# Two-layer directed graph network over 16 graphs: the mean is subtracted ahead of the closing root, and layer 1 spreads its row maxima one projection earlier

## What is computed

```
h = max(layernorm(x), 0)
for each of two layers:
    a    = softmax(h h^T / sqrt(384)) * adj
    attn = a / (rowsum(a) + 1e-10)
    ctx  = (attn above the diagonal) (h Wl^T + bl) + diag(attn) (h Ws^T + bs) + (attn below it) (h Wr^T + br)
    h    = max(layernorm(ctx) * g + beta, 0)
out = x + h
```

## Time and profile before

| | us |
|---|---|
| median of 3 runs | 1187.16 (1187.15 to 1187.18) |
| profiled execution, its own time | 1188.02 |
| its span in the profile | 1186.3 |
| TensorE busy | 1169.5 (99%) |
| VectorE busy | 1004.8 (85%) |
| GpSimd busy | 633.0 (53%) |
| ScalarE busy | 494.5 (42%) |

### The profile page before, as it was taken

The page is one execution under the profiler, slowest core; times in us unless marked ns, Lnnn a source line. Parts: engine busy times, 40 slices in busy tenths (PEclk is TensorE's granted clock), DMA queues, the critical chain, the costliest instruction groups (busy, mean ns, idle before and its releaser), DMA issues.

```text
span 1186.3 us, 18757 instructions
## 1 busy us (share of the span) xinstructions
PE 1169.5 (99%) x6998; PEld 1157.7 (98%) x6998; DVE 1004.8 (85%) x2064; ACT 494.5 (42%) x1065; POOL 633.0 (53%) x669
## 2 busy tenths in 40 slices
PE   9999999999999999999999999999999999999997
PEld 7999999999999999999999999999999999999997
DVE  6879987799877998779997798977989779895688
ACT  5346423364343543435434343344433454335532
POOL 3676454654545555455564455654556544654347
PEclk9999999999999999999999999999999999999999
DMA  6521312013120131211312112121222113110000
GB/s 226 203 65 54 115 54 81 19 54 116 54 81 19 54 115 55 80 36 55 97 54 81 37 63 90 58 76 37 83 70 80 54 36 104 48 54 1 1 27 27
DMA packets 43483, 80.57 MB, mean 68 GB/s; under 512 B 6912, under 2 KB 24832, under 8 KB 43392
## 3 DMA queue, kind: packets, MB, share of 16 engines
q1 hardware_dynamic: 43104, 78.98, 20.0%
q10 hardware_dynamic: 288, 0.39, 0.1%
HBM read 66.72 MB, written 12.64 MB: 67 GB/s over the span
## 4 chain that ended last, share of the span: by engine, by line
PE 54%; DVE 20%; POOL 10%; issue 10%; ACT 4%; DMA 1%; DVEq 0%; POOLq 0%
PE u_ps L337 9%; PE u_ps L339 9%; PE u_ps L338 9%; PE rot_ps L339 8%; PE rot_ps L338 8%; PE rot_ps L337 8%; POOL dg L957 4%; POOL hw_lo L945 4%; DVE et_lo L682 3%; DVE e_sb L677 3%; DVE xt_sb L665 3%; DVE proj L710 2%; DVE z L747 2%; DVE z L755 2%; ACT e_sb L515 2%
## 5 line engine op out<-in xcount | busy, mean ns | idle before, releaser
L945 POOL TENSOR_TENSOR hw_lo<-proj,hw_hi 128x384 fp32r<-128x384 f32 x256 | 283.1, 1126 | 242.3 <-ACT hw_hi L525 242.3
L337 PE MATMUL rot_ps<-w_hi,ht_hi 128*128 128x384 f32 x1152 | 389.3, 338 | 0.0
L339 PE MATMUL rot_ps<-w_hi,ht_lo 128*128 128x384 f32 x1152 | 385.4, 335 | 0.0
L338 PE MATMUL rot_ps<-w_lo,ht_hi 128*128 128x384 f32 x1152 | 385.2, 334 | 0.0
L338 PEld LDWEIGHTS rot_ps<-w_lo,ht_hi 128*128 128x128 f32 x1152 | 216.6, 188 | 0.0
L337 PEld LDWEIGHTS rot_ps<-w_hi,ht_hi 128*128 128x128 f32 x1152 | 216.5, 188 | 0.0
L339 PEld LDWEIGHTS rot_ps<-w_hi,ht_lo 128*128 128x128 f32 x1152 | 216.3, 188 | 0.0
L500 ACT ACTIVATE u_off<-u_ps 128x128 f32<-128x128 f32 (+1 forms) x128 | 42.4, 332 | 395.6 <-PE u_ps L339 395.4
L525 ACT ACTIVATE hw_hi<-proj 128x384 fp32r<-128x384 f32 x256 | 127.5, 520 | 78.1 <-DVE proj L710 78.1
L957 POOL TENSOR_TENSOR dg<-et_hi,tri 128x256 fp32r<-128x256 f32 x128 | 109.7, 857 | 89.9 <-PE u_ps L339 89.9
L710 DVE TENSOR_TENSOR proj<-rot_ps,bias 128x384 f32<-128x384 f32 x256 | 137.8, 548 | 21.9 <-PE rot_ps L339 21.8
(11 more groups left out here) (89 smaller groups left out, 2100.6 us busy)
## 6 DMA issues: line engine op xcount, KB each, us to landing
out_dram<-z SPq DMA_DIRECT2D x64, 192.0 KB, 1.9
x_norm<-x_dram SPq DMA_DIRECT2D x15, 768.0 KB, 4.5
xt_sb<-x_t_dram SPq DMA_DIRECT2D x15, 768.0 KB, 4.5
adj_a<-adj_t_dram SPq DMA_DIRECT2D x8, 1024.0 KB, 5.3
adj_b<-adj_t_dram SPq DMA_DIRECT2D x8, 1024.0 KB, 5.4
x_norm<-rows_dram SPq DMA_DIRECT2D x15, 512.0 KB, 3.8
x_a<-x_dram SPq DMA_DIRECT2D x8, 768.0 KB, 4.6
x_b<-x_dram SPq DMA_DIRECT2D x8, 768.0 KB, 4.7
```

The costliest lines, as they stand in the source:

```text
L337: pe.matmul(dst, a_hi, b_hi, start=first and m == 0, stop=False)
L338: pe.matmul(dst[:, 0:b_lo.shape[1]], a_hi, b_lo, start=False, stop=False)
L339: done = pe.matmul(dst, a_lo, b_hi, start=False, stop=last and m == n - 1)
L945: pool.tensor_tensor(hw_lo[:, t, n, :], proj[:, t % 2, n, :], hw_hi[:, t, n, 0:dim].bitcast(F32), ALU.subtract).then_inc(hw_lo_done, 1)
```

## The change

Four edits. In the unit list of layer 1, M stands behind three projections, (0,0), (0,1), (1,0), where it stood behind four. ScalarE copies the spread maxima before it rounds tile 0's projections. VectorE shifts the scores of tiles 0 and 1 before it reads out projection (1,1). GpSimd, in steps 1 and 3, does `x_centre` before `rstd_of`. No instruction is added or taken away.

```diff
-    UNITS_1 = [("P", *p) for p in PROJ[:4]] + [("M",)] + [("P", *p) for p in PROJ[4:] + SELF]
+    UNITS_1 = [("P", *p) for p in PROJ[:3]] + [("M",)] + [("P", *p) for p in PROJ[3:] + SELF]
...
                     for t in range(TILES):
                         row_sum(t)
+                    copy_max()
                     round_proj(0)
-                    copy_max()
                     exp(0)
...
                     evacuate(1, 0)
-                    evacuate(1, 1)
                     shift_scores(0)
                     shift_scores(1)
+                    evacuate(1, 1)
                     evacuate(2, 0)
...
-                rstd_of(slice(0, TILES), 1)
                 if s in (1, 3) and not last:
                     x_centre(it * 2 + (2 if s == 1 else 3))
+                rstd_of(slice(0, TILES), 1)
```

## The result

| | before | changed |
|---|---|---|
| median | 1187.17 us (6 runs, 1187.13 to 1187.80) | 1180.28 us (6 runs, 1179.88 to 1181.25) |
| profiled execution, its span | 1188.02, 1186.3 | 1179.88, 1178.1 |

The ratio is 0.9942, 95% interval 0.9929 to 0.9955: faster by 6.9 us, where 6.6 was forecast.

The account below looks back on a forecast made before the run. TensorE, busy 99% of the span, was taken as the bound. Terms of -3.85 (wait B), -3.85 (wait A), -0.1 (last pair) and +1.2 (M in step 3) gave -6.6 us: 1180.6 us, range 1179.0 to 1184.2.

Parts of the forecast that it names:

- What bounds: Whole kernel: TensorE is busy 99% of the span, so only its waits can be won, or new ones added.
- waits A and B: TensorE's waits, seven times 0.55 us each: A, step 2's transposes for a bank; B, step 0 for low parts.
- The subtraction ahead of the root costs nothing: Steps 1 and 3: GpSimd's 4.25 us of subtraction fit its 5.92 us idle gap, ending 1.7 us before `var_eps`.
- Wait B goes: Step 0 of the next pair: GpSimd's low parts end 2 us earlier, where 0.5 is needed; 7 x 0.55 = -3.85 us.
- Start of step 2: `x_scale` takes 1.88 us, VectorE waits for projection (0,0), and the maxima are 0.42 us ahead of M.
- How wait A goes: Step 2: earlier M and shifts give the read-out of (2,0) 0.75 us of lead; 7 x 0.55 = -3.85 us.
- M in step 3: Moved one projection earlier, M waits for the maxima 0.15 us in each of eight step 3: +1.2 us.
- The remainder of A in the last pair: Turns of step 2 in the last pair: a remaining wait of 0.1 us goes.
- Rival 1: Step 3: A's gain is given back to M, up to 0.55 us in seven pairs; 1184.4 at worst; chance 0.14.
- Rival 2: M becomes the bound in both steps, waiting 1.1 us in step 2; about 1188.2, no change; chance 0.05.
- Rival 3: The root waits behind the subtraction for the spread means; slower, 1194.5 with the load 2 us beyond slack; chance 0.03.
- Rival 4: The change does not reach TensorE: A and B find other releases just as late; 1188.4; chance 0.04.

Follow-up runs that it names:

- e3: The kernel before, with the mean subtracted ahead of the root in step 1 only; 1184.06 us, ratio 0.9975.
- e4: The kernel before, with the mean subtracted ahead of the root in step 3 only; 1183.92 us, ratio 0.9971.
- e1: The kernel before, with only the mean subtracted ahead of the root in steps 1 and 3; 1180.30 us, ratio 0.9942.
- e6: The changed kernel with ScalarE's copy and VectorE's read-out of (1,1) in their old orders; 1180.21 us, ratio 0.9941.
- e2: The changed kernel with the mean subtracted behind the root again, as before; 1191.44 us, ratio 1.0036.
- e8: e1 plus four unused GpSimd subtractions of 128x384 that read SBUF, behind the root of step 2; 1200.49 us, ratio 1.0111.

## Why the prediction was right

- **What bounds.** Right: waits A and B were all there was between the first pair and the tail, and e3 and e4 give each its size, 0.50 us (0.08 of A stays as long as M is not moved) and 0.54, for 0.55 read from the rows.
- **The subtraction ahead of the root costs nothing.** Right, with 2.17 and 1.54 us to spare for the 1.7 forecast. The `centre` beside it is stretched by 0.3 us, within the 1.4 allowed. In the first pair the root comes 1.1 us later, for up to 1.6 forecast, and nothing follows from it; but it is held by way of VectorE's `den`, not by GpSimd's own queue as the prediction had it.
- **Wait B goes.** Right; GpSimd's chain has 2.2 us of lead on the product, so it gained some 2.7, where I had estimated 2.
- **Start of step 2.** Right in what follows the change: scaling 1.89 us, VectorE waits 1.73 us for projection (0,0), the maxima are 0.4 us ahead of M. But the prediction had VectorE late by 2.2 us, from `x_scale` alone, and by contention. It was 3.4 us: `shift` was held for 1.1 us too, and much of the lateness of `x_scale` can be its dependence on the subtractions. As the change removes all of it, the sum did not suffer.
- **How wait A goes.** Here the reasoning credits the wrong edit. The prediction had A go by the lead that the earlier M and the earlier shifts give to the read-out of (2,0). e1 has neither, and A shrinks from 0.55 to 0.08 us all the same; e6 has the old order of copy and shifts, and A is gone. The moved subtraction is what removes A; the earlier M takes the last 0.08. The size of the term was right, since the change has both edits.
- **M in step 3.** The mechanism was right; the term was oversized. I had 8 x 0.15 = 1.2 us. Measured are 0.10 us each, and 0.27 in one pair: 1.0. The prediction took 0.14 us from an instruction's end to the start that it releases, from wait B; from the last maximum to M it is 0.06.
- **The remainder of A in the last pair** was 0.1 us, as forecast, and it too is gone.
- **The sum.** -6.6 forecast, -6.9 measured; the difference is less than two executions differ by at their start.

Rival 1 (A given back in step 3) did not happen: in the change M of step 3 starts 0.23 us after the matmul before it, and 0.22 in e2, where A is freed by M's own wait in step 2. Rival 2 did not happen here, but its price was about right: e2, without the moved subtraction, shows M's wait of 1.0 us in step 2, for 1.1. Rival 3 did not happen; both roots wait for `var_eps`. Rival 4 did not either: e3 and e4 show that each wait reaches the time. The chances of rivals 2 and 4 add up to 0.09, where the prediction put 0.08 for the two. What the prediction did not say, though its numbers held it, is that one of the four edits carries the whole gain: with the subtraction moved, what the earlier M wins in the turns (0.08 us a pair) and what it loses in step 3 (0.10) cancel.

What the runs do not settle: how much of VectorE's lateness in step 2, and so of wait A, was the collision and how much the dependence of `x_scale` on the subtractions; and what sets the differing start of an execution (0.5 to 1.65 us of wait for the first transposed rows), which no run varied.

## What to carry to other kernels

Where two engines slow each other, look for a stretch in which one stands idle waiting for the other anyway, and put there what it would do next; a queue position ahead of a wait is free as long as the work and its own waits fit into the gap, and what the other engine does in that gap can bear the collision. A unit pulled forward on the bounding engine must be judged in every step that it stands in: the same order gained in one step and lost in the next. And try the edits of a bundle alone; here one was the gain, two were nothing, and one was good in half of its places.

## What was unexpected of the hardware

Even a 128x4 instruction pays for the collision. The mean of 639 ns for `shift` in the kernel before mixes two cases: the seven that stand beside GpSimd's subtractions take 1.25 us each, the nine others 0.16, and in the changed kernel all take 0.16. GpSimd is slowed less than VectorE: in e8 a subtraction of 128x384 took 4.88 / 4 = 1.22 us, for 1.02 of a low part of that size in the earlier trace rows, beside VectorE's held instructions, each of which grew from about 0.6 to 1.4 us. And behind M's wait the next unit comes about 0.05 us later too (0.40 us from M to the next matmul for 0.36), so a wait of 0.05 us costs 0.10; behind the longer wait of M in e8 it is 0.11 us.
